# Slots 3, 4 and the tail of a gated-recurrence layer with a quantised feed-forward block, put in another order

## The reference

```python
# block 1, on layernorm(x)
pre = xn @ W + b                      # 256 -> 4*256: i, f, o, z
i_gate = 10 * tanh((i + input_bias) / 10); f_gate = -softplus(f)
o, tz = sigmoid(o), tanh(z)
m_next = max(f_gate + m, i_gate)      # recurrence over the 2048 steps
i_s, f_s = exp(i_gate - m_next), exp(f_gate + m - m_next)
c = f_s * c + i_s * tz;  n = f_s * n + i_s
h = o * (c / (n + 1e-6))
x1 = x + h / rms(h) * scale
# block 2, on layernorm(layernorm(x1))
y = silu(g @ w1 + b1)                 # w1, w2: (q - 128) * scales, int32 q
out = x1 + layernorm(x1) + 0.5 * (y @ w2 + b2)
```

## Time and profile before

| | us |
|---|---|
| runs | 343.87, 342.34, 343.74 (median 343.74) |
| profiled execution, whole | 342.19 |
| its span, first to last instruction | 340.4 |
| TensorE busy | 310.9 (91%) |
| VectorE busy | 262.7 (77%) |
| ScalarE busy | 229.1 (67%) |
| POOL busy | 154.7 (45%) |

### The profile page before, as it was taken

How to read it: one execution, slowest core, us unless ns; L and a number is a source line. 1 busy time by engine, 2 the same in 40 slices (tenths; PEclk the granted TensorE clock), 3 DMA queues, 4 the chain that set the end, 5 groups by cost and what they waited for, 6 DMA issues and landing times.

```text
span 340.4 us, 4803 instructions
## 1 busy us (share of the span) xinstructions
PE 310.9 (91%) x1760; PEld 269.2 (79%) x1760; DVE 262.7 (77%) x454; ACT 229.1 (67%) x368; POOL 154.7 (45%) x149
## 2 busy tenths in 40 slices
PE   0999999998949995969999999999999959999996
PEld 0788886886938885958899888988898849899895
DVE  3999997998977989598959986699669895662430
ACT  3499948799257961949795987779585773861830
POOL 2160050208960399921993179425943155265000
PEclk9999995899987999999999999999999978999999
DMA  7980000000000300002000200000000000100101
GB/s 274 368 315 2 1 0 2 0 0 0 2 1 2 123 1 0 3 31 94 0 0 34 92 0 2 31 34 0 0 2 31 34 0 0 64 0 3 62 1 64
DMA packets 10936, 14.22 MB, mean 42 GB/s; under 512 B 672, under 2 KB 10144, under 8 KB 10656
## 3 DMA queue, kind: packets, MB, share of 16 engines
q1 hardware_dynamic: 10496, 13.12, 11.0%
q10 hardware_dynamic: 416, 0.79, 0.6%
HBM read 9.71 MB, written 4.19 MB: 41 GB/s over the span
## 4 chain that ended last, share of the span: by engine, by line
PE 59%; DVE 20%; POOL 8%; ACT 6%; issue 5%; DMA 1%; DVEq 0%; POOLq 0%
PE mm_ps L209 10%; PE mm_ps L210 10%; PE mm_ps L211 10%; PE z_ps L209 6%; PE z_ps L211 6%; PE z_ps L210 6%; DVE y_lo L739 4%; POOL g L949 3%; POOL rec L925 2%; DVE rec L682 2%; DVE rec L693 1%; DVE rec L667 1%; PE t_ps L343 1%; DVE ve L727 1%; PE t_ps L329 1%
## 5 line engine op out<-in xcount | busy, mean ns | idle before, releaser
L209 PE MATMUL z_ps<-w_hi,y_hi 128*128 128x256 f32 x256 | 74.0, 289 | 4.4 <-DVE y_lo L739 3.8
L211 PE MATMUL z_ps<-w_hi,y_lo 128*128 128x256 f32 x256 | 72.9, 285 | 0.0
L210 PE MATMUL z_ps<-w_lo,y_hi 128*128 128x256 f32 x256 | 72.7, 284 | 0.0
L739 DVE TENSOR_TENSOR y_lo<-y,y_hi 128x512 fp32r<-128x512 f32 x64 | 48.6, 774 | 14.5 <-ACT y_hi L492 14.1
L209 PEld LDWEIGHTS z_ps<-w_hi,y_hi 128*128 128x128 f32 x256 | 48.9, 191 | 5.6 <-DVE y_lo L739 4.5
L489 ACT ACTIVATE y<-mm_ps,b_all 128x512 f32<-128x512 f32 x60 | 41.4, 690 | 13.6 <-PE mm_ps L278 9.0
L210 PEld LDWEIGHTS z_ps<-w_lo,y_hi 128*128 128x128 f32 x256 | 49.0, 191 | 0.1
L211 PEld LDWEIGHTS z_ps<-w_hi,y_lo 128*128 128x128 f32 x256 | 48.8, 191 | 0.0
L209 PE MATMUL mm_ps<-gt_hi,w_hi 128*128 128x512 f32 x108 | 44.1, 408 | 0.0
L210 PE MATMUL mm_ps<-gt_lo,w_hi 128*128 128x512 f32 x108 | 43.7, 404 | 0.0
L211 PE MATMUL mm_ps<-gt_hi,w_lo 128*128 128x512 f32 x108 | 43.5, 403 | 0.0
(11 more groups left out here) (144 smaller groups left out, 695.2 us busy)
## 6 DMA issues: line engine op xcount, KB each, us to landing
out<-rows SPq DMA_DIRECT2D x16, 256.0 KB, 2.1
rows<-x SPq DMA_DIRECT2D x7, 512.0 KB, 6.5
q<-fc_q SPq DMA_DIRECT2D x2, 1024.0 KB, 12.3
s<-fc_scales SPq DMA_DIRECT2D x1, 1024.0 KB, 11.5
wg_raw<-fc_scales SPq DMA_DIRECT2D x1, 1024.0 KB, 11.0
wg_raw<-w_gates SPq DMA_DIRECT2D x1, 512.0 KB, 5.6
wg_raw<-w_gates ACTq DMA_DIRECT2D x1, 512.0 KB, 6.0
rows<-x ACTq DMA_DIRECT2D x1, 256.0 KB, 3.6
```

Of the source, the lines that this page charges most:

```text
L209: pe.matmul(dst, wh[w_at], ah[a_at], start=start, stop=False)
L210: pe.matmul(dst, wh[w_at], al[a_at], start=False, stop=False)
L211: return pe.matmul(dst, wl[w_at], ah[a_at], start=False, stop=stop)
L739: dve.tensor_tensor(y_lo[:, j], y[:, j % YBUFS], y_hi[:, j].bitcast(F32), ALU.subtract).then_inc(y_lo_done, 1)
```

## The change

No instruction computes anything else than before; the order of the instructions on four engines and the engine of a few of them differ.

- TensorE: three tiles of fc2(0) stand ahead of g_turned(1) and one behind it, where all four stood ahead of it. In the tail two tiles of fc1(6) stand ahead of h_turned(7).
- ScalarE: g_normalised(1) is done here, not on POOL, ahead of x_normalised(4); g_high(1) goes ahead of reciprocal(2); g_high(0) goes ahead of a table load; square_sums(1) stands behind the first tile of gates(3). Slot 7 is written out: the table load, reciprocal(6) and exp_i(7) go ahead of g_high(5). In the tail square_sums(7) stands behind two tiles of silu(6).
- VectorE: input_times_z(2) and (7) and o_times_c(2), (6) and (7) are done here, not on POOL. denominators(1) goes ahead of b1_all; ln1_sums(4) and ln1_means(4) around mean_square(1); residual(1) behind w2_lo; h(2) between two y_low. Slot 7 is written out, with g_low(5) behind h(6), numerators(7) behind the last y_low(5), and g_low(6) between newton(7) and refined(7).
- POOL: base and base_bias of a chunk stand behind the roots of the next one in slots 3 and 4: base(0) behind ln2_root(1), base(1) behind ln2_root(2) and g_normalised(2), base(2) between rms_root(3) and ln2_root(3). From slot 5 the loop is as before. In slot 7 the two products are gone.

The diff; the lines of the TensorE, ScalarE, VectorE and POOL programs in this order:

```diff
@@ tensor @@
-            fc2(0, range(TT))
+            fc2(0, range(0, 3))
             g_turned(1)
+            fc2(0, range(3, TT))
             fc1(1, range(0, 2))
...
             fc2_both(5, 1)
+            fc1(6, range(0, 2))
             h_turned(7)
-            fc1(6, range(KF))
+            fc1(6, range(2, KF))
@@ scalar @@
             g_normalised(0)
+            g_high(0)
             act.preload_act_table_set("natural_log_exp_and_others")
-            g_high(0)
             reciprocal(1)
...
             silu_alone(0, range(4, KF))
+            act.preload_act_table_set("sigmoid_and_others")
+
+            gates(3, range(0, 1))
             square_sums(1)
-            act.preload_act_table_set("sigmoid_and_others")
-
-            gates(3, range(0, 4))
+            gates(3, range(1, 4))
...
             exp_i(3)
+            g_normalised(1)
             x_normalised(4)
+            g_high(1)
             reciprocal(2)
-            g_high(1)
             act.preload_act_table_set("silu_and_others")
...
-            for t in range(4, CHUNKS):
+            for t in range(4, CHUNKS - 1):
...
+            gates(7, range(GJ))
+            act.preload_act_table_set("natural_log_exp_and_others")
+            reciprocal(6)
+            exp_i(7)
+            g_high(5)
+            act.preload_act_table_set("silu_and_others")
+            square_sums(6)
+            silu(5, range(KF))
             g_normalised(6)
             act.preload_act_table_set("natural_log_exp_and_others")
             reciprocal(7)
             g_high(6)
             act.preload_act_table_set("silu_and_others")
+            silu(6, range(0, 2))
             square_sums(7)
-            silu(6, range(KF))
+            silu(6, range(2, KF))
@@ vector @@
+            def input_times_z(c):
+                r = rec[c % 2]
+                dve.wait_ge(i_ready, at(c, 1, 1))
+                dve.wait_ge(gate_done, at(c, 8, 6))
+                dve.tensor_tensor(r[:, 2], r[:, 2], r[:, 1], ALU.mult).then_inc(iz_ready, 1)
...
             maximum(1, range(1, KD))
+            denominators(1, range(KD))
             dve.wait_ge(beta_w1, 1)
...
-            denominators(1, range(KD))
             divisor(1)
...
             h(1)
+            input_times_z(2)
             y_low(0, range(0, 2))
...
+            ln1_sums(4)
             mean_square(1)
+            ln1_means(4)
             h_scaled(1)
-            residual(1)
             dve.wait_ge(w2_rounded, 1)
...
+            residual(1)
             ln2_sums(1)
             ln2(1)
-            ln1(4)
             maximum(2, range(KD))
             denominators(2, range(KD))
             divisor(2)
             numerators(2)
             g_low(1)
             newton(2)
+            o_times_c(2)
             refined(2)
-            y_low(1, range(0, 2))
+            y_low(1, range(0, 1))
+            h(2)
+            y_low(1, range(1, 2))
             x_low(4)
-            h(2)
...
-            y_low(5, range(4, 5))
+            y_low(4, range(6, KF))
+            denominators(6, range(KD))
+            divisor(6)
+            numerators(6)
+            o_times_c(6)
+            newton(6)
+            refined(6)
+            h(6)
+            g_low(5)
+            input_times_z(7)
+            maximum(7, range(KD))
+            final(4, 0)
+            denominators(7, range(KD))
+            divisor(7)
+            final(4, 1)
+            mean_square(6)
+            y_low(5, range(0, 1))
+            h_scaled(6)
...
+            y_low(5, range(4, KF))
             numerators(7)
-            y_low(5, range(5, KF))
+            o_times_c(7)
 
             newton(7)
+            g_low(6)
             refined(7)
             h(7)
-            g_low(6)
@@ gpsimd @@
-            pool.wait_ge(h_done, at(1, 1, 1))
-            input_times_z(2)
             rms_root(1)
+            ln1_root(4)
+            ln2_root(1)
             base(0)
             pool.wait_ge(b2_halved, 1)
             base_bias(0)
-            ln2_root(1)
-            g_normalised(1)
-            ln1_root(4)
-            o_times_c(2)
             pool.wait_ge(h_done, at(2, 1, 1))
             input_times_z(3)
             rms_root(2)
+            ln2_root(2)
+            g_normalised(2)
+            ln1_root(5)
             base(1)
             base_bias(1)
-            ln2_root(2)
-            g_normalised(2)
-            for t in range(4, CHUNKS):
...
+            o_times_c(3)
+            pool.wait_ge(h_done, at(3, 1, 1))
+            input_times_z(4)
+            rms_root(3)
+            base(2)
+            base_bias(2)
+            ln2_root(3)
+            g_normalised(3)
+            for t in range(5, CHUNKS - 1):
...
-            o_times_c(7)
+            base(5)
+            base_bias(5)
+            rms_root(6)
+            ln2_root(6)
             pool.wait_ge(h_done, at(7, 1, 1))
```

More of the change, by code:

```diff
@@ L557, in _ @@
             act.preload_act_table_set("sigmoid_and_others")
-            for t in range(4, CHUNKS):
+            for t in range(4, CHUNKS - 1):
                 gates(t, range(0, 7))
-                if exists(t + 1):
-                    x_normalised(t + 1)
+                x_normalised(t + 1)
                 gates(t, range(7, GJ))
@@ L567, in _ @@
                 exp_i(t)
-                if exists(t + 1):
-                    x_high(t + 1)
+                x_high(t + 1)
                 act.preload_act_table_set("silu_and_others")
@@ L851, in _ @@
             ln2(2)
-            for t in range(4, CHUNKS):
+            for t in range(4, CHUNKS - 1):
                 y_low(t - 3, range(6, KF))
-                if exists(t + 1):
-                    ln1(t + 1)
+                ln1(t + 1)
                 denominators(t - 1, range(KD))
@@ L864, in _ @@
                 h(t - 1)
-                if exists(t + 1):
-                    x_low(t + 1)
+                x_low(t + 1)
                 maximum(t, range(KD))
-                if not exists(t + 1):
-                    denominators(t, range(KD))
-                    divisor(t)
                 final(t - 3, 1)
@@ L880, in _ @@
                 ln2(t - 1)
-                if exists(t + 1):
-                    y_low(t - 2, range(4, 6))
-            y_low(5, range(4, 5))
+                y_low(t - 2, range(4, 6))
+            y_low(4, range(6, KF))
[16 more added lines that the diff above has]
+            h_scaled(6)
+            y_low(5, range(1, 2))
+            residual(6)
+            y_low(5, range(2, 3))
+            ln2_sums(6)
+            y_low(5, range(3, 4))
+            ln2(6)
+            y_low(5, range(4, KF))
             numerators(7)
-            y_low(5, range(5, KF))
+            o_times_c(7)
             newton(7)
+            g_low(6)
             refined(7)
             h(7)
-            g_low(6)
             final(5, 0)
@@ L1001, in _ @@
             rms_root(2)
+            ln2_root(2)
+            g_normalised(2)
+            ln1_root(5)
             base(1)
             base_bias(1)
-            ln2_root(2)
-            g_normalised(2)
-            for t in range(4, CHUNKS):
-                if exists(t + 1):
-                    ln1_root(t + 1)
+            o_times_c(3)
[7 more added lines that the diff above has]
+            for t in range(5, CHUNKS - 1):
+                ln1_root(t + 1)
                 base(t - 2)
@@ L1016, in _ @@
                 ln2_root(t - 1)
-                if exists(t + 1):
-                    g_normalised(t - 1)
-            o_times_c(7)
+                g_normalised(t - 1)
+            base(5)
+            base_bias(5)
+            rms_root(6)
+            ln2_root(6)
             pool.wait_ge(h_done, at(7, 1, 1))
```

## The result

The changed kernel takes 329.01 us (median of four runs, 328.28 to 330.61); the kernel before took 343.04 beside it (four runs). The ratio is 0.960, 95% interval 0.955 to 0.965. The profiled execution of the changed kernel took 329.68 us with a span of 327.7, where before it was 342.19 and 340.4. In a later set of runs the same kernel took 329.39 beside 342.39: 0.962 (0.960 to 0.964). The forecast was 330.0, range 326 to 336.

What follows compares the result with a forecast made beforehand. The prediction saw TensorE, busy 91% of the span, as the bound, with little to win outside its idle time and slow stretches. 1.2 + 8.5 - 0.4 + 3.7 = 13.0 off 342.19 gave 329.2; 0.8 for the clock made 330.0, range 326 to 336.

Steps and rivals of the forecast that it cites:

- Term 1: VectorE's chain up to w2_lo: w2_lo ends earlier, a gain of 1.2 us (0.5 to 2.4).
- Term 2: From w2_lo to g_turned(2): a gain of 8.5 us (5 to 10), gap A 7.2 and gap B 1.3.
- Gap A: TensorE's 5.1 us wait before fc1(1) for gt_hi, 7.2 with its low clock; forecast to go.
- Gap B: TensorE's 3.6 us wait before g_turned(2) for POOL's g; forecast to shrink to 2.3.
- Term 3: Slots 4 and 5: a loss of 0.4 us (0 to 2), from base(2) and base_bias(2) ahead of ln2_root(3).
- gap C: TensorE's 3.1 us wait before h_turned(3) for xt_lo; forecast to stay at 3.1.
- Term 4: The tail: g(7) is turned at 303.8 instead of 307.5, a gain of 3.7 us (2 to 6).
- Gap D: TensorE's 3.8 us wait in fc2_both(5, 0) for y_lo, 6.1 with its low clock; forecast to go.
- Rival 1: VectorE held more often, by moved products and bias additions; two more holds on the path give 334; chance 0.17.
- Rival 2: The tail gives nothing, its chain over h(7), base(6), base_bias(6), rms_root(7) no earlier: 333.7 us; chance 0.10.
- Rival 3: More than forecast: early clock rise, base_bias(0) out of VectorE's way, no fall at C: 326.1 us; chance 0.12.
- Rival 4: Slower: POOL's two-input instructions in the changed slots take VectorE over as the bound, 345.7 us; chance 0.04.

Runs made afterwards that it cites:

- den_early: The kernel before with one part of the change alone, denominators(1) ahead of b1_all: 340.92 us, ratio 0.9958 to the kernel before.
- fc2_whole: The changed kernel with all four tiles of fc2(0) ahead of g_turned(1): 328.36 us, ratio 0.9582 to the kernel before.
- the run with the roots first: The changed kernel with base(6) and base_bias(6) behind g_normalised(7) on POOL: 326.82 us, ratio 0.9535 to the kernel before.
- products_on_pool: The changed kernel with input_times_z(2) and o_times_c(2) back on POOL: 331.10 us, ratio 0.9671 to the kernel before.
- tail_as_before: The changed kernel with slot 7 and the tail in the old order on all four engines: 333.46 us, ratio 0.9736 to the kernel before.
- base0_ahead: The changed kernel with base(0) and base_bias(0) back ahead of ln2_root(1) on POOL: 330.09 us, ratio 0.9634 to the kernel before.
- g1_on_pool: The changed kernel with g_normalised(1) back on POOL, ahead of base(0): 333.38 us, ratio 0.9723 to the kernel before.

## Why the prediction was right, point by point

**Term 1** (w2_lo earlier; 1.2, bounds 0.5 to 2.4): fc2(0) came 2.5 us earlier. The chain was right to 0.2 us for the case with the early clock (82.1 forecast, 81.93 measured), and that case came. I had weighted it too low. (The prediction says that L925 ran in two thirds of the 3.48 us of y_lo; by the earlier trace rows it is 2.76, four fifths. Nothing in the sum rests on it.) The den_early run shows the single step behind it, with the same shorter low stretch. That the clock rises earlier because the idle 0.65 us is gone is likely, and not shown: all thirteen profiled executions with denominators(1) early had 6.8 us or less, but there is only one with the old order to set beside them, and in three of the thirteen the stretch was 3.4 us, so it also varies by execution.

**Term 2** (w2_lo to g_turned(2); 8.5): 47.7 us became 39.95, so 7.8. Gap A and its low clock went, as said. Two sizes were off. The pow of ln2_root(1) on POOL took 1.91 us beside VectorE's scans, where it had taken 1.04 in the kernel before, so g(1) was ready 7.8 us after w2_lo and not 7.0, still in time. base_bias(0) held VectorE by 2.2 us and not 1.3, at o_times_c(2) and not newton(2). Gap B was 2.43 for 2.3 forecast. h_turned(2) waited 0.24 for 0.4. Of this term's steps g(1) on ScalarE, fc2(0) split, base(0) behind the roots and the two products were each undone in a run; g_high(1) ahead of reciprocal(2) and w2_lo ahead of residual(1) were not.

**Term 3** (slots 4 and 5; a loss of 0.4): the loss was 1.6, and of another kind. The lateness that I feared from base(2) and base_bias(2) did not reach TensorE: there is no wait between h_turned(3) and the tail. The clock fell behind B and C, which the prediction had at 1.00 in the kernel before and named, as a fall in a new place, among the signs of being wrong. So this step came out wrong, though the total did not. What a fall costs depends on what comes next. From g_turned(2) to h_turned(3) it is 17.0 us in the changed kernel with a fall and 17.0 in the fc2_whole run without one (121.47 to 138.50): TensorE came later to a wait set by VectorE, and gap C shrank from 3.2 to 2.0. From h_turned(3) to gates(5) it is 13.75 with a fall and 12.25 without: 1.5 us lost. TensorE in the fc2_whole run:

```profile
138.50 1.16 PE L343 MATMUL t_ps<-ident,rec 128*128 128x128 f32 x8 [3.25 <-DVE xt_lo L633]
...
150.75 0.40 PE L243 MATMUL mm_ps<-xt_hi,wg_hi 128*128 128x512 f32 x1
```

The 0.8 us that I added to the forecast for the clock was to lie between the profiled execution and the median. It did not: the falls were in the profiled execution, 329.68 us for 329.2 forecast, and the median lies 0.7 us below it.

**Term 4** (the tail; 3.7): 4.1 by the two traces, 4.4 by the run that undoes it. Gap D is gone, the new waits stand where they were said to (1.2 us in fc2_both(6, 0), 0.7 at g_turned(7), which is less than the 1 to 3 us said), and what limits the tail is the POOL chain named, which the run with the roots first bears out by giving 2.5 us.

**Sum.** 2.5 + 7.8 - 1.6 + 4.1 = 12.8 for 13.0; the span shrank by 12.7. The errors of the four terms (+1.3, -0.7, -1.2, +0.4) cancelled; that the total is this near is partly luck.

**The rivals.** Rival 1 (VectorE held more often) happened in part: one hold larger than counted, 0.9 us. By the rule that the prediction took from the Trainium skill (SBUF — State Buffer, section "Who interferes with whom"), the products on VectorE would lock out POOL's base tiles. The trace agrees at the one place where they met: base(5)'s four tiles took 3.24 us beside o_times_c(6), and 2.17 in the kernel before. TensorE did not wait for it. base(0)'s tiles took 5.13 us beside the scans, but that is no price of the change (5.25 before), and products_on_pool shows that the products cost more from POOL. Rival 2 is out by tail_as_before. Rival 3 (more than forecast) came in terms 1 and 4 (2.5 and 4.1 for its 2.4 and 4.2) and not in terms 2 and 3. Rival 4 did not come near.

## What to carry to other kernels

Before moving work off a busy engine, look at what the same work does to it from its new place: here two products of 1.2 us each on VectorE replaced holds of 1.5 and 2.2 us that the same products on POOL gave VectorE. Put the long two-input instructions of the engine that holds others behind the short roots on the critical chain, and into a time in which the held engine waits for a third one or reads PSUM. (PSUM, because VectorE's x_low(4) and the final behind it, whose rows below show an operand in PSUM, took their usual 1.27 us for two beside POOL's product.) Time won ahead of such a hold is partly lost in it, so follow the chain to the next wait of the bounding engine before counting it.

```profile
103.07 2.77 POOL L963 TENSOR_TENSOR rec<-rec 128x1024 f32<-128x1024 f32 x1 [4.03 <-DVE rec L709]
...
103.52 1.27 DVE L634 TENSOR_TENSOR xt_lo<-t_ps,xt_hi 128x512 fp32r<-128x512 f32 x2
104.72 1.27 DVE L762 SCALAR_TENSOR_TENSOR rows<-z_ps,rows 128x512 f32<-128x512 f32 x2
```

## What the runs showed of the hardware that I had not expected

- A hold by POOL strikes scans too (4.54 us for 2.45, base0_ahead), as it does 4-element instructions (2.19 for 0.17) and 128x1024 products (3.41 for 1.21). In the other direction POOL's four tiles of g, 128x256 each, took 7.03 us beside scans (g1_on_pool) and 2.49 in the tail of the changed kernel.
- TensorE's clock does not follow the length of an idle gap alone: gaps of 3.6 and 3.1 us in the kernel before left it at 2.4 GHz, gaps of 2.4 and 2.0 us in the changed kernel were each followed by 3.4 us at 1.2 GHz, in both of its profiled executions, and gaps of 2.3 and 3.2 us in the fc2_whole run were not. The same gap of 3.6 us, in the same order of slot 4, was followed by no fall in the kernel before and by 6.8 us at 1.2 GHz in den_early. What decides it stays open here.
